# Adaptive-norm attention block with an MoE-LoRA FFN: another start of the program and another order in its last step and tail

## The reference, cut to what matters

```python
mod = (silu(c) @ wmod).reshape(4, 6, 1, -1)      # sa, ca, ga, sb, cb, gb
h = layernorm(x) * (1 + ca) + sa
w = codes * repeat(scales, 32, axis=0)           # for q, k, v, o
q, k, v = h @ wq + bq, h @ wk + bk, h @ wv + bv  # 16 heads of 128
attn = softmax(q @ k.T / sqrt(128)) @ v          # per batch and head
x = x + ga * (attn @ wo + bo)
h = layernorm(x) * (1 + cb) + sb
wmat = 16 * normalised_top2(softmax(h @ gate_w.T))     # 8 experts
lora = sum_e wmat[:, e] * (h @ A[e].T) @ B[e].T        # rank 16
x = x + gb * (h @ W.T + lora)
```

## Time and profile before

| | us |
|---|---|
| median of 3 runs | 777.58 (777.32 to 777.62) |
| profiled execution, its time | 777.42 |
| its span on the chip's clock | 775.5 |
| TensorE busy | 766.5 (99%) |
| VectorE busy | 647.5 (83%) |
| ScalarE busy | 517.6 (67%) |
| GpSimd busy | 483.4 (62%) |

### The profile page before, as it was taken

The page is one execution under the profiler, slowest core; times in us unless marked ns, Lnnn a source line. Parts: engine busy times, 40 slices in busy tenths (PEclk is TensorE's granted clock), DMA queues, the critical chain, the costliest instruction groups (busy, mean ns, idle before and its releaser), DMA issues.

```text
span 775.5 us, 14722 instructions
## 1 busy us (share of the span) xinstructions
PE 766.5 (99%) x4206; PEld 667.7 (86%) x4206; DVE 647.5 (83%) x1254; ACT 517.6 (67%) x1124; POOL 483.4 (62%) x454
## 2 busy tenths in 40 slices
PE   7999999999999999999999999999999999999998
PEld 6888888888888888888888888888888888888887
DVE  5889888888888888888888888888898888879876
ACT  2788676667666676667666766676667676766841
POOL 4686576548655675556657575655667476789722
PEclk9999999999999999999999999999999999999999
DMA  7554355444454335444445434543355334433202
GB/s 216 162 154 124 95 147 150 139 107 99 118 144 131 95 96 139 129 124 98 110 133 147 98 94 122 146 125 95 96 145 152 95 94 107 112 89 86 56 1 109
DMA packets 71898, 90.67 MB, mean 117 GB/s; under 512 B 19574, under 2 KB 37431, under 8 KB 71867
## 3 DMA queue, kind: packets, MB, share of 16 engines
q1 hardware_dynamic: 53184, 74.00, 37.3%
q10 hardware_dynamic: 18682, 16.30, 7.0%
HBM read 22.06 MB, written 2.11 MB: 31 GB/s over the span
## 4 chain that ended last, share of the span: by engine, by line
PE 95%; POOL 1%; DVE 1%; DMA 1%; ACT 1%; SPq 1%; issue 0%; DVEq 0%
PE score L1102 9%; PE score L1103 9%; PE score L1104 9%; PE qv L1102 8%; PE qv L1103 8%; PE qv L1104 8%; PE o L1102 7%; PE o L1104 7%; PE o L1103 7%; PE ky L1102 4%; PE ky L1103 4%; PE ky L1104 4%; PE y L1102 2%; PE y L1104 2%; PE y L1103 2%; DMA stage<-in_L_attn_wk_scales_dram 1%
## 5 line engine op out<-in xcount | busy, mean ns | idle before, releaser
L404 POOL TENSOR_TENSOR pT_lo<-pT,pT_hi 128x512 fp32r<-128x512 f32 x248 | 314.6, 1305 | 240.7 <-ACT pT_hi L576 240.6
L660 ACT ACTIVATE prob<-score,neg_max 128x512 f32<-128x512 f32 x256 | 172.7, 688 | 79.7 <-DVE neg_max L941 79.5
L941 DVE TENSOR_REDUCE neg_max<-score 128x1 f32<-128x512 f32 x256 | 159.7, 682 | 1.6 <-PE score L1104 1.6
L954 DVE STREAM_TRANSPOSE pB<-prob 128x512 f32<-128x512 f32 x252 | 156.4, 678 | 0.0
L576 ACT ACTIVATE pT_hi<-pT 128x512 fp32r<-128x512 f32 x248 | 135.3, 620 | 0.0
L1102 PE MATMUL score<-k_hi,q_hi 128*128 128x512 f32 x256 | 101.2, 395 | 0.6 <-DVE k_lo L862 0.6
L1103 PE MATMUL score<-k_lo,q_hi 128*128 128x512 f32 x256 | 100.3, 392 | 0.0
L1104 PE MATMUL score<-k_hi,q_lo 128*128 128x512 f32 x256 | 99.7, 389 | 0.0
L1102 PE MATMUL o<-pT_hi,v_hi 128*128 128x512 f32 x248 | 96.6, 389 | 0.0
L1104 PE MATMUL o<-pT_hi,v_lo 128*128 128x512 f32 x248 | 96.5, 389 | 0.0
L1103 PE MATMUL o<-pT_lo,v_hi 128*128 128x512 f32 x248 | 96.5, 389 | 0.0
(11 more groups left out here) (262 smaller groups left out, 1824.7 us busy)
## 6 DMA issues: line engine op xcount, KB each, us to landing
pT<-pB SPq DMA_DIRECT2D x1008, 64.0 KB, 2.0
out_dram<-x_nat SPq DMA_DIRECT2D x8, 256.0 KB, 2.1
stage<-in_L_attn_wv_codes_dram ACTq DMA_DIRECT2D x7, 256.0 KB
stage<-in_L_attn_wv_scales_dram ACTq DMA_DIRECT2D x14, 128.0 KB
stage<-in_L_attn_wq_codes_dram ACTq DMA_DIRECT2D x7, 256.0 KB
stage<-in_L_attn_wq_scales_dram ACTq DMA_DIRECT2D x14, 128.0 KB
stage<-in_L_attn_wk_codes_dram ACTq DMA_DIRECT2D x7, 256.0 KB
stage<-in_L_attn_wk_scales_dram ACTq DMA_DIRECT2D x14, 128.0 KB
```

Of the source, the lines that this page charges most:

```text
L404: pool.tensor_tensor(split(pT_lo, kt), turned(par, kt), split(pT_hi, kt).bitcast(f32), ALU.subtract).then_inc(p_lo_ok, 1)
L660: act.activation(prob[:, i], score_ps[i][:, :], ACT.Exp, bias=neg_max[:, i:i + 1], accum_out=row_sum[:, s % 2, i:i + 1]).then_inc(exp_ok, 1)
L941: dve.tensor_reduce(neg_max[:, i:i + 1], score_ps[i][:, :], AX.X, ALU.max, negate=True).then_inc(max_ok, 1)
L954: dve.transpose(pB[:, s % 2, :, i].rearrange("p g k q -> p k g q"), prob[:, i].rearrange("p (k g q) -> p k g q", k=QT, g=G)).then_inc(pB_o ...
```

## The change

**Scales.** The first block scales of q, k and v are loaded as rows (4 partitions, two halves) into cleared 128-row buffers by ScalarE's queue, and TensorE spreads them over the 32 partitions of each block: a matmul with a 0/1 block matrix that VectorE forms from the identity (`spread_rows`, two f32 calls of 256 columns a matrix). The product with the codes is formed by VectorE from the bank for all three. o's first scales are loaded as before.

**Order.** k is loaded, multiplied and projected ahead of q. Both first projections are done in two halves of 256 tokens with a bank each (y and o hold the second halves), and the hi and lo parts by half. The modulation comes in two chunks of features, each with its own bank, and the transposes of a chunk follow it directly, tile by tile. ScalarE forms the hi part of chunk 1 and evicts the bias vectors, which VectorE did. The idle transposes are 6 in place of 20, and the 14 and the 10 are gone. Batch 1 is normalised on VectorE within step 0, two tiles before the first turn and two after v_lo, and q_lo and k_lo now stand between the turns; batch 2's statistics follow input_hi.

**Last step and tail.** Batch 0's `lora_rows` uses the y bank in place of qv, so it need not wait for v_lo; v_lo comes behind the maxima; ScalarE evicts the FFN input first, and takes two of the pT_hi tiles ahead of o_hi; batch 1's statistics go ahead of the inverse. In the tail dense(1, 0) goes ahead of ffn_input(2), dense(1, 1) ahead of lora_rows(2), half of dense(3, 1) ahead of lora_transpose(0); ffn_input waits by bank; ScalarE takes batch 1's weighted rows ahead of the second `odds`.

```diff
+        def load_rows(queue, m):
+            src = bass.AP(SCALES[m].tensor, 0, [[FEAT, NB], [NB * FEAT, 2], [1, PW]])
+            queue.wait_ge(rows_zero, 1 + "kqv".index(m))
+            queue.dma_start(scale_rows[m][0:NB], src).then_inc(ld_rows[m], 16)
...
+            load_first(sp, "k")
             load_first(sp, "q")
-            load_first(sp, "k")
...
# gpsimd
             inverse_std(0)
+            parts("k", 0, 0)
             parts("q", 0, 0)
-            product("k", 0)
-            parts("k", 0, 0)
+            parts("v", 0, 0)
             parts("q", 0, 1)
             inverse_std(1)
-            product("v", 0)
-            parts("v", 0, 0)
             parts("k", 0, 1)
...
# scalar
             for c in range(DC):
+                modulation_out(c)
                 input_high(0, c, score_ps[2 + c])
+            act.wait_ge(h_ev, 2)
+            act.activation(hT_hi[:, 1, tokens(0)], hT32[:, 1], ACT.Copy).then_inc(h0_hi, 1)
...
-            q_high(1, 0)
-            k_high(1, 0)
-            normalise(1, range(QT))
+            for m in "kq":
+                for u in range(2):
+                    half_high(m, u)
...
+                    if end:
+                        ffn_input_out(0, 0, o_ps[0])
+                        ffn_input_out(0, 1, ky_ps)
                     if not start:
                         v_out(n + 1, batch_of(s) % 2, s % 2)
...
                     if end:
                         lora_out(0)
+                        prob_high((s - 1) % 2, landed(p, s - 1), end_hi[:, 0], range(2))
...
# vector
+            first_product("k")
+            first_product("q")
+            input_hi(0, 0)
+            input_lo(0, 0)
+            dve.wait_ge(ld_x[1], 16)
+            row_statistics(1, 0)
+            row_statistics(1, 1)
+            input_lo(0, 1)
+            first_product("v")
+            row_statistics(1, 2)
+            row_statistics(1, 3)
...
+                    elif start:
+                        normalise(1, range(2))
+                        turn(0)
+                        v_low(1, 0, 0, ky_ps)
+                        normalise(1, range(2, QT))
+                        q_low(n + 2, head_slice(p, s + 1))
+                        turn(1)
+                        k_low(n + 2, head_slice(p, s + 1))
+                        turn(2)
+                        turn(3)
+                        inverse()
+                        input_hi(1, 0)
+                        input_hi(1, 1)
+                        dve.wait_ge(ld_x[2], 16)
+                        statistics(2)
...
# tensor
-            for i in range(20):
+            for i in range(6):
                 pe.transpose(score_ps[0][:, (i % QT) * P:(i % QT + 1) * P], ident[:, :], ident[:, :])
+
+            def spread_rows(m):
+                pe.wait_ge(block_ok, 1)
+                pe.wait_ge(ld_rows[m], 16)
+                for c in range(2):
+                    ins = pe.matmul(first_scales(m)[:, c], block_rows[:, :, :].rearrange("a b q -> a (b q)"), scale_rows[m][:, c],
+                                    start=True, stop=True)
+                ins.then_inc(rows_mm[m], 1)
...
+            for u in range(DC):
+                for i, j in enumerate((SA + u, CA + u)):
+                    for c in range(DC):
+                        ins = pe.matmul(mod_banks[u][:, i * B:(i + 1) * B], wmod_1[:, c, j * P:(j + 1) * P], silu[:, c],
+                                        start=(c == 0), stop=(c == DC - 1))
+                ins.then_inc(mod_mm, 1)
+                for t in range(QT):
+                    pe.wait_ge(z_ok, t + 1)
+                    ins = pe.transpose(INPUT_BANKS[0][u][:, t * P:(t + 1) * P], z[:, 0, t, u * P:(u + 1) * P], ident[:, :])
+                ins.then_inc(h_tr, 1)
...
             lora_rows(1)
             dense(0, 1)
-            ffn_input(2)
             pe.wait_ge(y_ok, QT * (N - 1))
             dense(1, 0)
+            ffn_input(2)
+            dense(1, 1)
             lora_rows(2)
-            dense(1, 1)
             ffn_input(3)
             pe.wait_ge(y_ok, QT * N)
             dense(2, 0)
             lora_rows(3)
             dense(3, 0)
             pe.wait_ge(ag_ev, QT * B)
+            dense(3, 1, (2,))
             lora_transpose(0)
-            dense(3, 1)
+            dense(3, 1, (3,))
             lora_transpose(1)
```

228 lines of the change are left out of this document (131 added, 97 removed).

## The result

The new kernel's median is 779.62 us (19 executions, 776.67 to 781.85) against 777.68 for the kernel before (19 executions, 777.13 to 778.26) beside it: ratio 1.0022, interval 1.0014 to 1.0030. It is slower by 0.2%, where 775.6 and at most 777.3 were forecast. Six further executions gave 780.92, ratio 1.0043 (1.0029 to 1.0058). The profiled execution of the new kernel is the fastest of its 19, 776.67 with a span of 774.9, so there are two questions: why even this one gained only 0.75 us on the profiled execution before (777.42) and not 1.85, and what made the others up to 5 us longer.

A forecast was written before the change was run, and what follows sets the result against it. TensorE, busy 99% of the span, was taken as the bound, leaving only the beginning and the last 50 us. Gains of 1.6 and 0.25 us, 1.85 off 777.42, gave 775.6; range 774.5 to 777.3.

The forecast's parts named there:

- First scores at 17.6: Start: step 0's first scores begin near 17.6 instead of 20.43, a lead of 2.8 us.
- VectorE's q_lo as TensorE's wait ahead of v's projection of step 1: Step 1: TensorE reaches v's projection at 35.9 and waits 0.6 us for VectorE's q_lo.
- The landing as the last thing ahead of pT_hi: Step 0: pT_hi starts right after the transposed probabilities land, at 39.2 instead of 40.69, 1.5 us earlier.
- No hole before ffn_input(2): Tail: dense(1, 0) fills TensorE's wait before 747.69, worth 0.6 us with the issue slots.
- What VectorE gives back: Steps 0 and 1: VectorE's added work puts the last turn at 27.4, cutting TensorE's 2.8 us lead to 2.15.
- Rival A: Start: clock doesn't rise at 14.2, half matmuls run slower, scores' lead 1.4, only the tail gains: 777.1; chance 0.2.
- I take the same rise: Start: TensorE's clock rises to 2.4 GHz near 14.2 as before, despite 6 idle transposes instead of 44; no cost.
- Rival C: Start: clock stays low through first scores and v's projection, if TensorE has wider holes before the scores: 780.0; chance 0.06.
- The tail: Last 50 us: last step and FFN together gain 0.25 us, bounds -0.6 to 0.7.
- Last step: Last step: earlier lora rows gain 0.35, eaten by two pT_hi tiles ahead of o_hi; net 0.1 us lost.
- FFN: FFN: closed wait gives 0.6, ffn_input(3)'s chunk 1 waits 0.25 for ScalarE's logits copy; net 0.35 us gained.

The follow-up runs named there:

- the two places mended: New kernel with step 0's first turn ahead of batch 1's first z tiles and the eps addition behind step 1's maxima: 778.29 us, 1.0008.
- the last two kernels: New kernel with VectorE's two reorderings and six transposes before step 1's v projection: 778.47 us, 1.0015; also with later loads held and the old tail: 778.02, 1.0006.
- the eight transposes': New kernel with eight idle transposes between q's halves and step 0's first scores: 779.77 us, 1.0031 to the kernel before.
- the hold: New kernel with SP's loads from batch 1's rows on issued only once the first modulation block has landed: 778.31 us, 1.0013 to the kernel before.
- the moved spread: New kernel with v's spread moved between the second half's modulation columns and its input transposes: 781.59 us, 1.0050 to the kernel before.
- the second mended tail: Old start with the new last step and tail, but all four pT_hi tiles behind o_hi and dense(1, 1) split around lora_rows(2): 777.77 us, 1.0000.

## Why the prediction was wrong, step by step

**What held.** *First scores at 17.6*: 17.46 in the first profile, and 17.43 to 17.81 in all six profiles with this order and the short low stretch. The lead of 2.8 was 2.97. Part of that hit is luck: v's spread was forecast to hold TensorE to 13.6 and k's halves begin at 12.34, but nine or ten of the half matmuls then run at half clock, not three or four; the two errors about cancel. *VectorE's q_lo as TensorE's wait ahead of v's projection of step 1*: it is there, 0.71. *The landing as the last thing ahead of pT_hi*: 0.16 by the row. *No hole before ffn_input(2)*: closed.

**What VectorE gives back: mis-sized, 1.2 forecast (2.8 to 1.6) and 2.05 measured (2.97 to 0.92).** Forecast was a last turn at 27.4; it ended at 28.2. Of the 6.05 us allowed from the last maximum (21.35) the row shows 7.1 (21.09 to 28.2): z took 2.37, not 1.6, because its first two tiles ran into GpSimd's weight product (1.52 for what takes 0.84), and VectorE waited 0.45 for k_hi, which TensorE's own wait for v_lo had made late. Then hT_hi to v_lo was taken at 2.8 and was 3.06: the statistics were over at 30.7, and the eps addition was then held by GpSimd's hT_lo for another 0.5; with the addition moved away the chain takes 2.37 (29.51 to 31.88 in that profile). Before, it took 1.93 (30.13 to 32.06), since only one of the four row statistics stood behind the cast there, and the addition met GpSimd's first tile and not its second. That the term does not depend on the lead is seen in every profile with this order and no second fall: step 2's scores 23.25 to 23.52 us behind the first, against 21.47 to 21.63 in four profiles of the old start. With the two places mended it is 22.08, twice. At step 3's scores 0.92 of lead is left where 1.6 was forecast; these 0.68 us and 0.47 in the tail (below) are why even the fastest execution lies 1.1 us above the forecast.

**The shape of the sum was wrong too.** Rival A took the give-back as a limit ("nothing is left but the tail", 777.1): with less lead at the first scores the landing would come as before. It is a delay instead: between step 0's scores and step 2's the new kernel takes 1.8 us more than the old one, whatever the lead is. With first scores at 19.27 the lead is 1.16, and at step 2's scores it is -0.68 (42.59 against 41.91). So A's price was near (1.4 forecast; of the 1.81 between the two profiles about 0.26 is the later landing, the second eight columns starting at 9.77 and not 9.51, and 1.55 the longer low stretch), its result was not: it ends on the slower side. Its reason, fewer idle transposes, isn't borne out either: the old start has the double stretch as well. (With VectorE's places mended the landing acts as a limit as well: see the last two kernels.)

**The clock: the step that failed.** "I take the same rise" went by the one profiled execution, and put the term at nothing. The give-back and the tail make 1.1 us of the miss (776.67); the other 3 us, up to the median of 779.62, come with the first low stretch and the second fall. The rise differs between executions; in the twelve profiles with the new start the first low stretch ended at 13.9 to 14.8 in seven and at 15.25 to 16.8 in five. What the old start showed for it was next to nothing, as its path there was k's scales, GpSimd and VectorE (0.13 us later in the profile above, 0.2 between the medians at 0.996 and 0.998). Taking these off the path put TensorE's 24 half matmuls on it, and with them every variation of its clock. With the new start the same two clocks lie 1.1 us apart where the second fall is absent. That the old start's times are narrow could not show this. (The forecast's reading that transposes don't keep the clock down set four-number columns against transposes, 0.13 against 0.21 us each; like against like came only here, eight columns in 1.05 and in 1.68, and bears it out.) The waits before the fall differ as well: the columns waited 0 to 1.79 us for the modulation's block, and of the five profiles with 0.69 or more in the new kernel's order four had the long stretch; but so had one with no wait (the eight transposes').

**Rival C** (0.06) came about in a form that the text didn't have: not the first scores and v at half clock, but a second fall near 40, behind the holes 0.69, 0.73 and 0.71. Its condition named holes ahead of the scores; the ones that counted come behind them. Three of the nine new-start profiles without transposes in the last hole have the fall, and about a third of their executions its clock (33 of 93), against a chance of 0.06. Size: 1.4 us. Together: 776.67 + 1.81 + 1.4 = 779.9, against a median of 780.08 for the ten executions at 0.991 to 0.993. The executions of 781.5 and more are not explained by this sum.

**The tail: 0.25 of gain forecast, about 0.2 of loss measured.** From the last step's scores to the last residual the 13 profiles with the new tail or parts of it take 51.25 to 51.59, the three with the old one 51.16 to 51.23. *Last step*, 0.1 of loss forecast: the lead goes from 0.92 to 0.70 (735.22 before, 734.52 after). The pT_hi tiles wait 0.84 for the landing and stand ahead of o_hi, as said, and the out projection's lead is down to 0.78 (730.64 before); the rest goes on VectorE's last lo part. The mechanism was right, its size 0.22, but it was not alone: with those tiles back behind o_hi, VectorE's last lo part still left no gain. *FFN*, 0.35 of gain forecast: the hole goes, and the second chunk of ffn_input(3) waits for its bank by 0.28 (753.28 is 0.71 behind the first chunk at 752.57, where before they stood 0.43 apart), near the 0.25 of the forecast. What the sum had left out is another 0.3 us in small waits between 759 and 768, around the LoRA transposes and the last dense halves. From 734.5 on the lead is 0.70 at the end as at the start: 0. The medians (1.0006 and 1.0000, intervals of 0.0018) can't tell either from nothing, so this rests on the profiles alone.

**What stays open.** What decides in an execution whether the low stretch is the short or the long one: the hold and the moved spread didn't settle it, and the eight transposes stood too late to. How the loss divides between the two stretches: filling the last hole alone gave no better median (778.47 against 778.29, 11 executions each), filling all three gave 778.34 against the new kernel's 779.62, and intervals of 0.0018 to 0.0020 (1.4 to 1.6 us) can't rank them. No kernel here removed the first stretch. And why the two kernels with the hold lost 0.4 to 0.5 between step 3 and the last.

## What to carry to other kernels

A lead won on one engine's path is worth only what the next in line lets through: read from the trace which engine becomes last, and whether what it varies in (here TensorE's granted clock at a start full of waits and tiny matmuls) was hidden until now. One profile can't show that variation; the run-to-run times of the old kernel don't either, because the old path hid it. The mean clocks of its executions do: 26 of 116 had double the low time at 0.2 us. A give-back through a serial chain of engines is first of all a delay to subtract from every case, and not only a limit that a large lead meets.

## What the runs showed of the hardware

- Some VectorE instructions on SBUF tensors wait for GpSimd's running elementwise one: a copy of 8 elements 1.26 us, an addition to 4 elements 1.20 and 0.65 (0.16 to 0.17 alone), two z tiles (scalar_tensor_tensor) 1.52 (0.85 alone). Row statistics (1.40 for four beside GpSimd, 1.39 alone) and turns (1.29 for two from 24.06 in the kernel before, beside GpSimd's wk_lo and product, as elsewhere) don't. v_lo, which reads PSUM, ran at its 0.68 beside GpSimd before the change (32.06, while hT_lo ran from 30.63 for 2.74).
- Behind waits of 0.7 us on TensorE in an otherwise full stretch the granted clock fell to 0.50 in three of nine profiles, at a cost of 1.4 us; with six idle transposes in the last hole none of three profiles shows it, and none of 33 executions has a mean clock of 0.994 or less (33 of 93 without them).
- The low stretch at the start was 3.4 us long in some executions and 6.8 in others of one kernel (3.41 and 6.83 in the new kernel's two profiles), and with the old start too (3.41 in the kernel before, 6.83 in the second mended tail).
- The record of the granted clock can begin with a rise: half-pace columns (1.87 us for eight, 1.05 elsewhere) under a recorded 1.00.
